# Paired half-height inverse products, gate work between the Gram products, and the heads' softmax inside the inverse transform

## What is computed

```
xf     = fft2(x)                                   # per channel, 128 x 128
qf     = xf.reshape(b, 8 heads, 16, h*w);  qn = qf / |qf|
attn_f = einsum('bhcn,bhdn->bhcd', qn, qn) * temp_f
attn_f = complex(softmax(attn_f.real), softmax(attn_f.imag))
out_f  = abs(ifft2(einsum('bhcd,bhdn->bhcn', attn_f, qf)))
g      = relu(batchnorm(conv1x1(xf.real, w1)))     # 128 -> 8 channels: "hidden"
g      = sigmoid(conv1x1(g, w2))                   # 8 -> 128 channels: the gates
out_f_l= abs(ifft2(g * xf))
```

## Time and profile before

| | us |
|---|---|
| median of 3 runs | 25445.41 (25442.5 to 25447.85) |
| profiled execution, its own time | 25446.71 |
| its span from first to last instruction | 25444.9 |
| mean granted clock of TensorE | 0.953 |

### The profile page before, as it was taken

One profiled execution on the slowest core, in us unless ns is written; L12 is line 12 of the kernel. 1 busy time (PEld: TensorE's weight loads), 2 busy tenths in 40 slices (PEclk: granted clock), 3 DMA queues, 4 the chain that ended last, 5 costly groups with the idle time before them and its releaser, 6 DMA issues.

```text
span 25444.9 us, 329441 instructions
## 1 busy us (share of the span) xinstructions
PE 22919.1 (90%) x107489; PEld 13392.0 (53%) x107489; DVE 20005.1 (79%) x23961; ACT 13236.0 (52%) x18799; POOL 12338.9 (48%) x4613
## 2 busy tenths in 40 slices
PE   5999989999998989998888888888888888888888
PEld 3776768677776868676333333333333333333333
DVE  3665746465664746567999999999999999999999
ACT  2323132322313132232777777777777777777777
POOL 0000000000000000001999999999999999999998
PEclk7999999999999999999999999999999999999999
DMA  2122130302222130213444444444444444444444
GB/s 83 53 81 77 56 103 28 98 35 86 71 80 79 38 114 20 86 46 110 165 167 189 170 167 189 167 191 167 165 191 165 170 191 166 191 168 166 190 167 163
DMA packets 866693, 3187.54 MB, mean 125 GB/s; under 512 B 68265, under 2 KB 340026, under 8 KB 579770
## 3 DMA queue, kind: packets, MB, share of 16 engines
q1 hardware_dynamic: 866234, 3181.65, 33.9%
HBM read 2884.91 MB, written 296.49 MB: 125 GB/s over the span
## 4 chain that ended last, share of the span: by engine, by line
PE 33%; DVE 8%; issue 6%; ACT 3%; DMA 2%; DVEq 0%; ACTq 0%; POOL 0%; SPq 0%; POOLq 0%
PE yp L2037 16%; PE pj L1993 8%; DVE hid L2260 4%; DVE hid L2266 3%; PE pj L2022 2%; PE pj L2052 2%; PE pj L2010 2%; PE pj L2001 2%; PE yp L2029 2%; ACT t L2119 1%; DMA img<-x 1%; DVE delta L2302 1%; ACT xn L2133 1%; DMA bc<-bc_rows 1%; ACT du L2167 1%
## 5 line engine op out<-in xcount | busy, mean ns | idle before, releaser
L2368 POOL TENSOR_TENSOR hid<-hid,bc 128x2048 f32<-128x2048 f32 x2048 | 7814.2, 3816 | 917.9 <-DVE carry L2274 914.9
L2037 PE MATMUL yp<-hid,ident 128*128 128x512 f32 x16384 | 7345.3, 597 | 430.4 <-POOL hid L2368 430.2
L2342 POOL TENSOR_SCALAR_AFFINE_SELECT ident<-ident 128x128 f32<-128x128 f32 x1 | 0.3, 293 | 11925.9 <-DVE ident L2227 11925.9
L2037 PEld LDWEIGHTS yp<-hid,ident 128*128 128x128 f32 x16384 | 3040.4, 189 | 4631.0 <-issue 3948.8
L2260 DVE TENSOR_TENSOR_SCAN hid<-da,carry,t 128x512 f32<-128x512 f32 x3968 | 4855.8, 1265 | 110.9 <-DVE carry L2274 15.9
L2266 DVE TENSOR_TENSOR_SCAN hid<-t,carry,hid 128x512 f32<-128x512 f32 x3968 | 4826.2, 1257 | 37.1 <-ACT t L2108 35.1
L2361 POOL TENSOR_TENSOR hid<-bc,du 128x1024 f32<-128x1024 f32 x2048 | 4101.0, 2002 | 200.9 <-PE yp L2037 174.5
L2108 ACT ACTIVATE t<-delta,v_a 128x512 f32<-128x512 f32 x4096 | 2659.9, 681 | 1569.0 <-DVE hid L2266 1565.9
L1201 PE MATMUL bk<-region 128*128 128x256 f16 (+2 forms) x30640 | 3380.9, 266 | 80.6 <-ACT region L1547 44.9
L1993 PE MATMUL pj<-xn,w_x 128*128 128x512 f32 x4096 | 2384.3, 736 | 1090.9 <-ACT xn L2133 1043.5
L1201 PE MATMUL bk<-work,region 128*128 128x256 f16 x27336 | 3180.0, 275 | 23.6 <-DVE region L1046 20.4
(11 more groups left out here) (288 smaller groups left out, 23056.1 us busy)
## 6 DMA issues: line engine op xcount, KB each, us to landing
bc<-bc_rows SPq DMA_DIRECT2D x1024, 2048.0 KB, 7.2
work<-in_shift_d SPq DMA_DIRECT2D x256, 512.0 KB, 3.8
work<-in_x SPq DMA_DIRECT2D x256, 256.0 KB, 2.7
work<-in_x SPq DMA_DIRECT2D x128, 512.0 KB, 5.1
xpad<-in_x SPq DMA_DIRECT2D x32, 2048.0 KB, 12.3
gated<-work SPq DMA_DIRECT2D x256, 256.0 KB, 2.2
region<-gated SPq DMA_DIRECT2D x256, 256.0 KB, 2.9
region<-heads SPq DMA_DIRECT2D x256, 256.0 KB, 3.1
```

The source lines that it names most:

```text
L2037: m = nc.tensor.matmul(yp[:, h, :], ident[:, :], hid[:, k % 4, n, :], start=False, stop=(g == G - 1 and n == 3), skip_group_check=True)
L2368: nc.gpsimd.tensor_tensor(hid[:, k % 4, :, :], hid[:, k % 4, :, :], bc[:, g, 1, :, :], ALU.mult).then_inc(s_hc.sem, 1)
```

## The change

- PE: `hidden_rows` (one step of stage 3) becomes a function. Steps 0 and 1 are issued ahead of the wait for the finished spectrum, the steps 2 to 7 behind the Gram parts 0 to 5. ACT copies hidden steps 0 and 1 ahead of its first column copy, and then two steps ahead of each further one.
- DVE, PE and ACT: the heads' softmax chain moves behind the gates. On DVE it stands behind line 863's instruction; on PE `f_rows` behind the fifth inverse2 pair and `f_soft` behind the tenth; on ACT the square root behind the second pair of absolute values and the exponential behind the seventh.
- PE: `inverse2` takes both halves at once, with the products of the two row halves alternating, each half in a bank of its own (four banks in place of two). `inverse1` comes in twos, ACT's copies and absolute values too.

```diff
@@ vector @@
                 dve.wait_ge(s_gp.sem, s_gp.at(b, NGC))
+                (the loop of the s_h1 copies, the loop of the gate products
+                 and the first column's two fixes, unchanged, moved up here)
                 G = bk[6]
...
                 mark("f_mix")
-                (from here)
@@ tensor @@
+                pe.wait_ge(s_xn.sem, s_xn.at(b, 4))
+                def hidden_rows(q):
+                    pe.wait_ge(s_t8c.sem, s_t8c.at(b, q - 1))
+                    if q >= 2:
+                        pe.wait_ge(s_t8st[q % 2], b * 256 + 64 * (q // 2))
+                    for i in range(4):
+                        r = 2 + 16 * q + 4 * i
+                        m = mm(bk[q % 2][32 * i:32 * i + JG, :], w1t[:, :], xpad[:, r:r + 4, 2:2 + P], start=True, stop=True)
+                    m.then_inc(s_t8.sem, 1)
+                hidden_rows(0)
+                hidden_rows(1)
                 pe.wait_ge(s_xr.sem, s_xr.at(b, NK + 1))
...
                 for k_ in range(NGC):
                     gram_part(k_)
-                (the eight hidden steps, f_rows and f_soft)
+                    if k_ < 6:
+                        hidden_rows(k_ + 2)
...
-                def inverse2(t):
-                    pe.wait_ge(s_z.sem, s_z.at(b, t // 2 * 2 + 2))
-                    pe.wait_ge(s_abs.sem, s_abs.at(b, t - 1))
-                    r = slice(64 * (t % 2), 64 * (t % 2) + 64)
-                    mm(bk[2 + t % 2][:, :], k["back"][r, 0:P], Z[r, t // 2 % 2, :, 0:P], start=True, stop=False)
-                    mm(bk[2 + t % 2][:, :], k["back"][r, P:], Z[r, t // 2 % 2, :, P:], start=False, stop=True).then_inc(s_i2.sem, 1)
+                def inverse2(s):
+                    pe.wait_ge(s_z.sem, s_z.at(b, 2 * s + 2))
+                    pe.wait_ge(s_abs.sem, s_abs.at(b, 2 * s - 2))
+                    for part, first in ((slice(0, P), True), (slice(P, 2 * P), False)):
+                        for hf in range(2):
+                            r = slice(64 * hf, 64 * hf + 64)
+                            m = mm(bk[2 + 2 * (s % 2) + hf][:, :], k["back"][r, part], Z[r, s % 2, :, part], start=first, stop=not first)
+                            if not first:
+                                m.then_inc(s_i2.sem, 1)
...
+                for s in range(NK // 2):
+                    if 2 * s + 2 < NK:
+                        inverse1(2 * s + 2)
+                        inverse1(2 * s + 3)
+                    inverse2(s)
+                    if s == 4:
+                        small_mm(VL["f_rows"], (bk[7][:, 0:P], k["ones"], diag[:, 0:P]))
+                    if s == 9:
+                        pe.wait_ge(v.sem, v.at(b, VL["f_soft"]))
+                        mm(bk[7][:, 0:P], sq[0], k["mixc"], start=True, stop=True)
+                        mm(bk[7][:, P:2 * P], sq[0], k["mixs"], start=True, stop=True).then_inc(m_.sem, 1)
@@ scalar @@
-                for k_ in range(1, NGC, 2):
-                    turn_columns(k_)
                 for q in range(8):
                     act.wait_ge(s_t8.sem, s_t8.at(b, q + 1))
                     cp(hidden[:, q % 2, :], bk[q % 2][:, :]).then_inc(s_t8c.sem, 1)
-                    if q == 4:
-                        small_act(VL["f_root"], col(10), col(8), ACT.Sqrt)
-                small_act(VL["f_max"], sq[0], sq[1], ACT.Exp, bias=col(15), accum_out=col(16))
+                    if q % 2 == 1:
+                        turn_columns(q)
...
                 zcopy(0)
+                zcopy(1)
+                for s in range(NK // 2):
+                    if 2 * s + 2 < NK:
+                        zcopy(2 * s + 2)
+                        zcopy(2 * s + 3)
+                    for g in (2 * s, 2 * s + 1):
+                        (wait s_i2 at g + 1, wait for the store of g - 2 as before)
+                        cp(Yb[:, g % 2, :, :], bk[2 + g % 4][:, :].rearrange("p (c w) -> p c w", c=4), ACT.Abs).then_inc(s_abs.sem, 1)
+                    if s == 1:
+                        small_act(VL["f_root"], col(10), col(8), ACT.Sqrt)
+                    if s == 6:
+                        small_act(VL["f_max"], sq[0], sq[1], ACT.Exp, bias=col(15), accum_out=col(16))
```

More of the change, by code:

```diff
@@ L818, in image @@
                 dve.wait_ge(s_gp.sem, s_gp.at(b, NGC))
+                for hf in range(2):
+                    dve.wait_ge(s_h1.sem, s_h1.at(b, hf + 1))
+                    src = bk[2 + hf][:, :].rearrange("p (j u) -> p u j", j=4)
+                    link(V.tensor_copy(A8[:, :, 4 * hf:4 * hf + 4], src[:, 0:HALF, :]))
+                    V.tensor_copy(B8[:, 1:64, 4 * hf:4 * hf + 4], src[:, HALF:, :]).then_inc(s_h1c.sem, 1)
+                for g in range(NUG):
+                    dve.wait_ge(s_sig.sem, s_sig.at(b, 4 * g + 4))
+                    n_u = min(UG, U64 - g * UG)
+                    if n_u < UG:
+                        for i in range(2):
+                            V.tensor_tensor(XLAST[:, i, :], XLAST[:, i, :], gates2[g % 2][:, n_u, :], ALU.mult).then_inc(s_gx.sem, 1)
+                    for X in (XR, XI):
+                        part = X[:, :, g * UG:g * UG + n_u]
+                        V.tensor_tensor(part, part, gates2[g % 2][:, 0:n_u, :].rearrange("p u c -> p c u"), ALU.mult).then_inc(s_gx.sem, 1)
+                dve.wait_ge(s_gx.sem, s_gx.at(b, 2 * NUG + 2))
+                V.tensor_tensor(XR[:, :, 0], XR[:, :, 0], XLAST[:, 1, :], ALU.subtract).then_inc(s_gx.sem, 1)
+                V.tensor_tensor(XI[:, :, 0], XI[:, :, 0], XLAST[:, 0, :], ALU.add).then_inc(s_gx.sem, 1)
                 G = bk[6]
@@ L844, in image @@
                 mark("f_mix")
[L845 to L863, removed]
                 def turned_rows(kk):
@@ L1617, in image @@
                             act.wait_ge(s_yst[g % 2], b * (8 * NK) + 16 * (g // 2))
-                        cp(Yb[:, g % 2, :, :], bk[2 + g % 2][:, :].rearrange("p (c w) -> p c w", c=4), ACT.Abs).then_inc(s_abs.sem, 1)
+                        cp(Yb[:, g % 2, :, :], bk[2 + g % 4][:, :].rearrange("p (c w) -> p c w", c=4), ACT.Abs).then_inc(s_abs.sem, 1)
[3 more added lines that the diff above has]
+                        small_act(VL["f_max"], sq[0], sq[1], ACT.Exp, bias=col(15), accum_out=col(16))
                 def take_rows(kk):
```

## The result

| | before | after |
|---|---|---|
| median of runs, us | 25443.96 (4 runs) | 25005.50 (4 runs, 25001.5 to 25008.18) |
| span of the profiled execution | 25444.9 | 25006.4 |
| mean granted clock | 0.953 | 0.957 |

The ratio is 0.9828 (95% interval 0.9811 to 0.9845), 438 us less.

The account below looks back on a forecast made before the run. No engine was seen as busy throughout; the bound changes by stage, PE in Gram and inverse, DVE in gates. Gains of 21.2 (hidden steps) and 26.9 us (inverse) times 8 images, 385 us, gave 25062 from 25446.7, range 25020 to 25130.

Parts of the forecast that it names:

- So the second half can start at 0.21: Paired inverse2: the second half starts 0.21 us after the first, making a pair 2.12 us and a period 5.77.
- the tail: End of the old inverse stage, chunks 29 and 30: read as overlapping halves with an offset of at most 0.8 us.
- The rival with 0.76: Inverse2 pairs: the halves' offset is 0.76 us as at the old stage's end, giving 25122 us; chance 13%.
- the one in program order: Inverse2 pairs: products start and end in program order, period about 5.99 us, giving 25085 us; chance 10%.
- A part and a step, 5.04 us: Gram stage on PE: a part of 3.84 us plus a hidden step of 1.2, two shape changes included.
- The clock of part 0: Gram part 0, 7.0 us before, could take anywhere from 7.0 to 3.9; the middle was taken, 1.5 us less.
- The start and end of the inverse stage: Inverse stage: 9.8 us before the first inverse2 pair, and 4.9 from pair 14's end to the last absolute value.
- the path from h1 to the first gate product: Stretch between hidden steps and gates: 3.5 us off 14.0, as PE comes straight from work.
- part 7's wait: Last Gram part: with no hidden step ahead of it, it waits 0.7 us for ACT's column copy.
- no wait for the turned load or a store: Hidden steps among Gram parts: no step waits for a store, and the turned load hides by 0.3 us.
- the small products: Inverse stage on PE: two records for f_rows and four for f_soft add 0.7 us to the path.
- The clock rival: Inverse stage: the fuller array brings the granted clock to the lower level, slower at 25770 us; chance 2%.

Follow-up runs that it names:

- the order experiment: The changed kernel with each inverse2 pair issued as both products of rows 0 to 63, then both of rows 64 to 127: 25002.3 us, ratio 0.9829.
- late Gram parts keep TensorE awake: The changed kernel with hidden steps earlier, Gram parts 6 and 7 behind all gate logits, held until gate products of groups 2 and 3 finish: 24930.2 us, ratio 0.9797.

## Why the prediction was wrong, step by step

The two stages' gains were 24.0 and 31.1 us an image (from line 785 to the first gate product 75.06 to 51.11, from the first inverse1 to the next stage's first copy 125.07 to 94.01), forecast as 21.2 and 26.9. The stages shrank in the ways that I gave. The sum was short by 6.9 us an image because one delay in it, that the second half's weight loads queue behind the first's, doesn't exist, and because its other sizes erred to the same side.

- **"So the second half can start at 0.21" is the term that failed most.** By the records' starts it was 0.01 us, so 0.2 x 15 = 3.0 us an image, 24 in all. I had reasoned from weight loads 0.11 apart within one half that those of the other half queue behind them. They don't: four lie where two did, in all 112 pairs between groups of inverse1. The hidden steps had shown it, and the tail that seemed to contradict was a wait on a copy, as the order experiment and ACT's row show. The rival with 0.76 falls for that reason. So does the one in program order: in the half-after-half kernel the second half's first product starts 0.01 us after the first half's first, while that half's second product, which stands ahead of it in the program, starts 0.96 us later. By the Trainium skill (TensorE: Matmul & The Clock Gate, "The mechanism" of Part 3) products would start and end in program order. The trace disagrees, and the measurement decides.
- **A part and a step, 5.04 us, was 4.75.** I took the modelled length of a part, 3.84, which runs beyond the start of what follows, and added two changes of shape of 0.2. The parts start 3.77 before the step and the step 0.98 before the part, changes included: a load of 8 columns exposes next to nothing. From part 0's end to h1 32.9 us for 34.8: 1.9 an image, 15 in all.
- **The clock of part 0**: "anywhere from 7.0 to 3.9, I take the middle". In five of eight images it ran at the upper level throughout; 2.1 us gained for 1.5, 5 in all. That number is partly luck: in the six experiments whose steps 0 and 1 stand at the same place it did so in 6, 6, 4, 3, 2 and 4 of eight images.
- **The start and end of the inverse stage** came 0.7 and about 0.4 shorter: the first pair 9.1 us after the first inverse1 for 9.8 (8.6 to 10.0 over the images, so more of those records ran at the upper level than in the kernel before). With the pairs alone it was 9.7, near the forecast, and 9.2 to 9.5 in the others that have both edits (8.4 where late Gram parts keep TensorE awake). What brings the difference no run isolates.
- **Right**: the path from h1 to the first gate product (10.5 forecast, 10.4 measured), the gates' unchanged 30.3, part 7's wait (0.7 forecast, 0.57), no wait for the turned load or a store (the load lands 0.9 us before h1), the small products (0.7 forecast; from the first pair to the last record 81.7 us for 81.1 with the pairs alone), the softmax chain hidden in the inverse stage, ACT's loads of tables hidden there, the Relu without a load of its own.
- **The range** was too narrow below. I had given each low bound (no offset 3.1, full clock 1.6) but stopped at 25020 where these two alone gave 38 us under 25062, that is 25024. Nothing stood for an error in the spacing of parts. And the earlier trace rows supported the bound better than the value I took.
- **Slips that change nothing above.** "A pair of steps takes PE 1.05 us" is one step, as the sum then has it. The rival of the tail's offset counts 14 pairs where 15 pay: 25128, not 25122. The clock rival turns the gain into a loss at 54% of the stage, not 60%.
- Per image the stretch gained 55.0 us and the whole image 54.1 (1456.6 to 1402.6), so something is given back behind the inverse stage. From the next stage's first copy to line 785 of the next image 1225.8 us passed before and 1227.2 pass now, 1227.4 with the pairs alone, 1226.2 with the hidden steps alone and 1225.3 with the halves kept apart (means of seven images). It is not a longer wait for the next stage's first shift matrix: up to 11 us behind that copy the rows stand where they stood. Of the 1.3 us 0.7 arise between 11 and 21 us behind it, and there the clock differs: from 11 to 15 us the granted clock was 1.00 in six of eight images before and in two after, and 0.63 to 0.68 in the other six. Why, no run shows.

## What to carry to other kernels

When two estimates for an overlap differ, look for the wait in the one that shows less: the list of what an instruction waits for tells more than its neighbours' spacing. Price insertions by the distance from start to start, not by modelled lengths. And moving a stage into a gap uncovers whatever had been lying beside it: the hidden steps gained 92 us alone and some 190 with the softmax chain moved along.

## What the runs showed of the hardware

- Two float32 products of 64 rows each, in the two halves of the array and in different banks, start 0.01 us apart and both take the time of one, in either program order (a pair 1.92 us, one alone 1.91). Taking the overlap away cost 231 us for 128 pairs, 1.8 us each, of which 0.2 is the wait that did it.
- Here a change between full-height, half-height and 8-column products costs about 0.1 us, plus the first weight load of the new shape where that is long (0.11 us for 128 columns).
- TensorE's granted clock at the start of a stage depends on small work before it, and not the same way each time. With 2 us of 8-column products in an idle stretch of 4.6 us, part 0 ran at 2.4 GHz throughout in 30 of 56 images (2 to 6 of the eight in each of seven traces); with the same products directly before it in 4 of 8; without them, in the kernel before and in the pairs alone, in none of 16.
